# TensorE's order in a fused token, attention and FFN kernel: two instead of three regions of array halves, and the first FFN product one step later

## The chip, the cores and the metric

One core of a Trainium2 chip runs the whole program. The metric is the device time of one execution in microseconds (us), median of several runs. The profiled execution has a time of its own, and its span (first to last instruction) lies within that time. TensorE is PE, its weight loader PEld, VectorE is DVE, ScalarE is ACT, GpSimd is POOL, and SyncE is SP, whose queue (SPq) issues the DMAs.

## What is computed

The input x is 64 sequences of 256 rows of 192 numbers, f32. Three layers follow each other, the last two with a residual and a layer norm ahead of them:

```python
h = tok(x, tok_Wq, tok_bq, tok_Wkv, tok_bkv)   # per sequence: 16 blocks of 16 rows; 8 queries, keys, values
                                               # per block, softmax of 8 x 8, out = q + attn v -> 128 rows
h = h + attn(layernorm(h), Wq, Wk, Wv, Wo)     # 12 heads of 64, 3 key/value heads, rope, softmax; 64 x 128
                                               # rows make (64, 128, 192), each sequence attends within itself
h = h + gelu(layernorm(h) @ in_weight.T + in_bias) @ out_weight      # 192 -> 768 -> 192
```

The output is 64 x 128 x 192.

## The kernel before, in words

The 64 sequences are worked on in 32 pairs (NP = 32). Every engine runs the same software pipeline: step p does the attention of pair p (att), the token layer of pair p + 1 (tok), the end of the attention and the FFN of pair p - 1 (ffn), and the second FFN product of pair p - 2 (fin). Steps -1, 0 and 1 fill the pipe, steps 2 to 30 are the loop, steps 31 to 33 empty it. The order of the work on each engine is written out by hand, in that engine's function step; the engines meet by semaphores alone, so an engine that waits holds up all that stands behind it.

The names that matter, for PE: qk_projected(0..3) and v_projected project queries, keys and values (f32r matmuls of 256 columns, 10 to each part); tok_qk projects the token layer from x_sb and waits for x_loaded; tok_scores, tok_mix and tok_h are the rest of the token layer; scores(a) are the attention scores of sequence a of the pair, probs_v(a) its value product, output(a) the product with Wo; x_turned and hn_turned transpose the normalised rows; ffn_first and ffn_second are the FFN's products. scores uses halves of the array's rows; probs_v, tok_scores and tok_h use halves of its columns; all else uses the full array. A "region of array halves" is an uninterrupted stretch of such matmuls.

On ACT stand the exponentials (score_exp), copies out of PSUM (v_out_of_psum, heads_out, h_added), gelus, and the first part of each f32r split (x_hi, h_hi). On DVE: the rotations' first half (rotate), key_max, the second part of each split (x_lo, h_lo), the norms, and blocks_turned(a, k), which transposes 32 x 32 blocks of the probabilities E into EB. On POOL: the rotations' second half (8 pieces to a pair), the normalisation of the probabilities (probs), the powers of the norms.

Probabilities must be transposed for the value product. DVE turns the blocks, SP writes EB to a DRAM buffer (3 spills), waits for them to land and reads them back in block order into ET (8 loads); this is blocks_moved(a, q). The x of the next pair has one buffer, x_sb: load_ahead(n) waits until tok_h of pair n - 1 has read it. In a loop step SP runs these in this order:

```python
blocks_moved(1, p - 1)
blocks_moved(0, p)
load_ahead(p + 2)
store(p - 2)
```

In blocks_moved all three spills stand ahead of the first load of ET, so the loads wait for blocks_turned(a, 2) to be done as well. PSUM has eight banks: two rings of three (RING[0], RING[1]) and B6, B7. Which product may run where is set by who still reads a bank: tok_qk writes into RING[1], whose second bank also holds the last two of the six hidden blocks (HIDDEN[2]), so it waits for gelus.

In the loop, PE's step 2 to 30 before is: projections 0 and 1, tok_qk, projections 2 and 3, values; one piece of ffn_second; probs_v(0), tok_scores, scores(0); output(0); probs_v(1); a piece; tok_mix; output(1); pieces; tok_h, scores(1); a piece; hn_turned; pieces; ffn_first(0), x_turned, ffn_first(2, 1).

Of the kernel before, what the change touches and what calls it, by code (L numbers as in the profile page):

```python
# [63 lines left out]
GELU_ORDER = (4, 5, 0, 1, 2, 3)  # L64
FFN_BANKS = {True: (0, 2, 1), False: (0, 1, 2)}
# [25 lines left out]
def program(nc, x, w_tok, b_tok, bq_row, bv_row, w_att1, w_att2, wo, w_in1, w_in2, b_in, w_out,  # L91
# [4 lines left out]
    with ExitStack() as ctx:  # L96
# [10 lines left out]
        TOK_S, TOK_M, TOK_H = RING[1][:, 512 + DP:512 + DP + P], B7[:, 0:DP], RING[0][:, 512:512 + 2 * D]  # L107
# [6 lines left out]
        FIRST_T = (B6[:], B7[:], RING[0][:, 1024:1536])  # L114
# [41 lines left out]
        v_tok, v_late, OT = sb("v_tok", [P, 2, DKV]), sb("v_late", [P, DKV]), sb("OT", [P, 2, DQ])  # L156
# [10 lines left out]
        s_keys = sem("s_keys")  # L167
# [26 lines left out]
        norm_out, first_mm, first_out = sem("norm_out"), sem("first_mm"), sem("first_out")  # L194
# [39 lines left out]
        def _(sp):  # L234
# [40 lines left out]
            def step(p, att, ffn, fin, more):  # L275
                if ffn and not (isinstance(p, int) and p == NP):
                    blocks_moved(1, p - 1)
                if isinstance(p, int) and p == 0:
                    for k in range(3):
                        sp.sem_inc(spilled[k], 16)  # L280
                    for k in range(2):
                        sp.sem_inc(filled[k], 64)
# [11 lines left out]
            for dst, src in ((smask, c_mask), (ident, c_ident), (rope_kc, c_rope_kc), (rope_ks, c_rope_ks),  # L294
# [16 lines left out]
        def _(act):  # L311
# [13 lines left out]
            def step(p, att, tok, ffn, fin):  # L325
                n = p + 1
                att_first = isinstance(p, int) and p == 0
                att_last = isinstance(p, int) and p == NP - 1
                main = att and fin
# [16 lines left out]
                def v_out_of_psum():  # L346
                    need(act, pv_mm, 4 * (p - 1) + 2)
# [24 lines left out]
                def first_copied(k):  # L372
                    g = GROUPS[k]
                    s0, heads = PIECES[g // 2]
                    h0 = REP * g - s0
                    act.wait_ge(first_mm, k + 1)
                    nc.scalar.copy(
                        ET[:, 0, s0 * P:(s0 + heads) * P].rearrange("p (i h c) -> p h i c", i=NB, h=heads)[:, h0:h0 + REP],
                        FIRST_T[k].rearrange("p (h i c) -> p h i c", h=REP, i=NB)).then_inc(first_out, 1)

# [13 lines left out]
                def v_kept_late():  # L394
                    act.wait_ge(v_out, p + 1)
                    need(act, pv_mm, 4 * p)
                    nc.scalar.copy(v_late[:], v_tok[:, 1]).then_inc(v_kept, 1)
# [14 lines left out]
                def exp_warmed():  # L412
                    act.wait_ge(s_warm_exp, p + 1)
                    nc.scalar.activation(warm[:, 1:2], half_neg[:, 0:1], ACT.Exp).then_inc(s_warm_exp, 1)

                def gelus():
                    act.wait_ge(s_warm, p)
                    nc.scalar.activation(warm[:, 0:1], warm[:, 0:1], ACT.Gelu).then_inc(s_warm, 1)
                    for m in GELU_ORDER if att else range(NM):
                        act.wait_ge(hid_mm, 3 * (p - 1) + FFN_BANKS[main].index(m // 2) + 1)  # L420
# [3 lines left out]
                if main:  # L424
                    exp_warmed()
                    bias_summed()
                    v_out_of_psum()
                    heads_out(p - 1, HEADS_0)
                    if tok:
                        token_exp()  # L430
                    for k in range(NKV):
                        score_exp(0, k)
                    residual_kept()
                    if tok:
                        h_added()
                    v_kept_late()
                    h_normalised()
                    residual_moved()
                    h_hi()
                    score_exp(1, 0)  # L440
                    score_exp(1, 1)
# [972 lines left out]
```

## Time and profile before

| | us |
|---|---|
| median of 3 runs | 946.08 (945.1 to 946.31) |
| the profiled execution's own time | 945.8 |
| its span | 943.8 |
| PE busy | 914.4 (97% of the span) |
| DVE / ACT / POOL busy | 761.9 / 639.6 / 666.1 |
| TensorE's granted clock, mean | 0.994 |

The rows below come from three kinds of view. A row of the timeline gives the start and the length of an instruction or of a group of like ones (x12 is twelve), and in brackets how long the engine was idle before it and who released it. Matmuls overlap their neighbours, so the distance from one start to the next is what a matmul takes of PE's time, not its length. A row of the stretches gives the busy time of each engine in a stretch, and the clock granted in it (1.00 is 2.4 GHz, 0.50 is 1.2 GHz). A row of the waits gives who waited for whom, in total, with count and longest.

### The profile page before, as it was taken

How to read it: one execution, taken by the hardware profiler on the slowest of the kernel's cores; microseconds unless marked ns; L12 is line 12 of the kernel's file. 1: busy time of each engine (PE TensorE's matmuls, PEld its weight loads, DVE VectorE, ACT ScalarE, POOL GpSimd, SP SyncE). 2: the span in 40 equal slices, each digit the busy share in tenths (PEclk: the TensorE clock that was granted, in tenths of full speed). 3: DMA queues.
4: the chain of work that ended last, by engine and by line, in shares of the span. 5: the costliest groups of instructions: out<-in, count | busy, mean ns of one | idle time of the engine just before them, and what ended most of it. 6: DMA issues, size and time to landing. Idle time of an engine off the chain costs nothing.

```text
span 943.8 us, 26528 instructions
## 1 busy us (share of the span) xinstructions
PE 914.4 (97%) x7722; PEld 799.7 (85%) x7722; DVE 761.9 (81%) x1999; ACT 639.6 (68%) x2501; POOL 666.1 (71%) x968
## 2 busy tenths in 40 slices
PE   5779999999999999999999999999999999999998
PEld 3567998888998888988888889888899888899877
DVE  3787888888888888888888888888888888888863
ACT  2556676667677667677667768666767766767763
POOL 2686677787667787667777767777766778766771
PEclk8999999999999999999999999999999999999999
DMA  6034644445545444554444554444564444555440
GB/s 205 24 91 135 165 126 126 131 121 153 164 138 131 122 131 134 164 149 134 116 127 131 162 161 123 126 131 126 153 164 132 130 126 126 141 164 147 114 118 21
DMA packets 193424, 124.63 MB, mean 132 GB/s; under 512 B 30976, under 2 KB 184960, under 8 KB 193408
## 3 DMA queue, kind: packets, MB, share of 16 engines
q1 hardware_dynamic: 190528, 121.02, 46.8%
q10 hardware_dynamic: 2880, 3.41, 1.1%
q8 instruction: 8, 0.13, 0.1%
q14 instruction: 8, 0.07, 0.0%
HBM read 69.32 MB, written 55.05 MB: 132 GB/s over the span
## 4 chain that ended last, share of the span: by engine, by line
PE 93%; DVE 3%; issue 1%; ACT 1%; DMA 1%; POOL 1%; SPq 0%; ACTq 0%; DVEq 0%; POOLq 0%
PE ring L1043 15%; PE bank L1062 14%; PE ring L1081 11%; PE bank L1260 7%; PE ring L1260 6%; PE ring L1117 6%; PE ring L1161 5%; PE ring L1021 4%; PE ring L1167 3%; PE bank L1117 3%; PE ring L1186 3%; PE ring L1221 3%; PE bank L1161 2%; PE ring L1198 2%; PE bank L1167 2%; PE bank L1242 2%
## 5 line engine op out<-in xcount | busy, mean ns | idle before, releaser
L335 ACT ACTIVATE E<-ring,m_neg 128x128 f32<-128x128 f32 x768 | 270.5, 384 | 17.3 <-DVE m_neg L688 16.9
L546 POOL TENSOR_TENSOR E<-E,e_rcp 128x512 f32<-128x512 f32 x158 | 177.8, 1126 | 85.6 <-DVE e_rcp L711 83.1
L538 POOL TENSOR_TENSOR qkT<-rot_c,rot_s 128x256 f32<-128x256 f32 x256 | 187.3, 732 | 20.1
L335 ACT ACTIVATION_READ_ACCUMULATOR E<-ring,m_neg 128x1 f32 x768 | 171.0, 223 | 0.0
L536 POOL TENSOR_TENSOR rot_s<-rot_s,rope_qs 128x256 f32<-128x256 f32 x192 | 143.3, 746 | 20.2 <-DVE rot_s L682 20.2
L1062 PE MATMUL bank<-wout_sb,G 128*128 128x192 f32 x744 | 152.0, 334 | 0.0
L688 DVE TENSOR_REDUCE m_neg<-ring 128x4 f32<-128x512 f32 x192 | 127.4, 678 | 21.3 <-PE ring L1081 21.3
L1062 PEld LDWEIGHTS bank<-wout_sb,G 128*128 128x128 f32 x744 | 118.7, 190 | 15.2 <-issue 11.5
L702 DVE STREAM_TRANSPOSE EB<-E 128x512 f32<-128x512 f32 x186 | 126.0, 692 | 1.6 <-POOL E L546 0.8
L1081 PE MATMUL ring<-qkT 64*128 64x128 f32 x1536 | 103.0, 280 | 2.2 <-POOL qkT L538 0.7
L1081 PEld LDWEIGHTS ring<-qkT 64*128 64x128 f32 x1536 | 91.6, 187 | 14.6 <-issue 13.1
L349 ACT COPY v_tok<-ring 128x384 f32<-128x384 f32 x32 | 15.3, 479 | 118.2 <-PE ring L1117 111.7
L682 DVE STREAM_SHUFFLE rot_s<-ring 128x512 f32<-128x512 f32 x128 | 94.6, 739 | 0.0
L355 ACT COPY h_next<-ring 128x384 f32<-128x384 f32 x32 | 15.3, 479 | 97.6 <-PE ring L1221 97.5
L680 DVE TENSOR_TENSOR rot_c<-ring,rope_qc 128x512 f32<-128x512 f32 x96 | 65.4, 681 | 16.9 <-PE ring L1043 16.9
L1043 PE MATMUL ring<-XH,WH 128*128 128x256 f32 x256 | 74.9, 293 | 1.9 <-ACT XH L410 1.4
L536 POOL TENSOR_TENSOR rot_s<-rot_s,rope_ks 128x256 f32<-128x256 f32 x64 | 46.6, 729 | 38.8 <-DVE rot_s L682 38.7
L1043 PE MATMUL ring<-XL,WH 128*128 128x256 f32 x256 | 71.7, 280 | 0.8 <-DVE XL L771 0.8
L1043 PE MATMUL ring<-XH,W2S 128*128 128x256 f32 x256 | 71.6, 280 | 0.0
L1043 PE MATMUL ring<-XL,W2S 128*128 128x256 f32 x256 | 71.6, 280 | 0.0
L1043 PE MATMUL ring<-XH,WL 128*128 128x256 f32 x256 | 71.5, 279 | 0.0
L1260 PE MATMUL bank<-wo_sb,OT 128*128 128x192 f32 x384 | 70.8, 334 | 0.7 <-ACT OT L343 0.7
(160 smaller groups left out, 2476.8 us busy)
## 6 DMA issues: line engine op xcount, KB each, us to landing
spill<-EB SPq DMA_DIRECT2D x186, 256.0 KB, 2.3
ET<-spill SPq DMA_DIRECT2D x248, 128.0 KB, 2.8
ET<-spill SPq DMA_DIRECT2D x248, 64.0 KB, 2.4
x_sb<-in_x_dram SPq DMA_DIRECT2D x64, 192.0 KB, 2.5
out_dram<-out_sb SPq DMA_DIRECT2D x31, 192.0 KB, 2.5
x_sb<-in_x_dram SPq DMA_DIRECT2D x64, 64.0 KB, 2.4
w_raw<-in_w_att_dram ACTq DMA_DIRECT2D x2, 608.0 KB, 5.2
win_raw<-in_w_in_dram ACTq DMA_DIRECT2D x2, 384.0 KB, 6.4
```

The lines of the kernel that those rows point to most:

```text
L335: last = nc.scalar.activation(E[:, a, s * P:(s + 1) * P], RING[a][:, s * P:(s + 1) * P], ACT.Exp, bias=m_neg[:, a, s:s + 1], accum_out=e_s ...
L536: nc.gpsimd.tensor_tensor(rot_s[:, b, :, a], rot_s[:, b, :, a], sin, ALU.mult).then_inc(sin_out, 1)
L538: nc.gpsimd.tensor_tensor(qkT[:, b, :, a], rot_c[:, b, :, a], rot_s[:, b, :, a], ALU.add).then_inc(q_out, 1)
L546: nc.gpsimd.tensor_tensor(e, e, r, ALU.mult).then_inc(prob_out, 1)
L682: nc.vector.stream_shuffle(rot_s[:, b].rearrange("p c a t -> p (c a t)"), src, SWAP).then_inc(rot_out, 1)
L688: nc.vector.tensor_reduce(m_neg[:, a, REP * g:REP * (g + 1)], RING[a][:, 512 * g:512 * (g + 1)].rearrange("p (h k) -> p h k", k=P), AX_X, ...
L702: nc.vector.transpose(EB[:, a, s0 * P:(s0 + heads) * P].rearrange("p (j h c) -> p h j c", j=NB, h=heads)[:, h0:h0 + REP], E[:, a, 512 * g: ...
L1043: last = nc.tensor.matmul(RING[0][:, 512 * (i % 2) + half * DP:512 * (i % 2) + (half + 1) * DP], w[:, c], r, start=(k == 0), stop=(k == 4))
L1062: last = nc.tensor.matmul(y, G[:, m, a * P:(a + 1) * P], wout_sb[:, m, :], start=(m == 0), stop=(m == NM - 1))
L1081: last = nc.tensor.matmul(RING[a][:, s * P:(s + 1) * P], qkT[rows, t // 2, t % 2, a], qkT[rows, 3, h // 8, a], start=True, stop=True)
L1117: last = nc.tensor.matmul(dst[k * HD:(k + 1) * HD], v[:, g * HD:(g + 1) * HD], src.rearrange("p i h c -> p i (h c)"), start=True, stop=True)
L1260: last = nc.tensor.matmul(y, OT[:, a, t * P:(t + 1) * P], wo_sb[:, t, :], start=(t == 0), stop=(t == 5))
```

## The change

It moves work on every engine. The second FFN product of pair p - 2 stays in step p; the first one (and the gelus) of pair p - 2 now also stand in step p, at its head, where before they stood at the end of step p - 1. x_turned moves ahead of the last pieces of ffn_second, tok_qk behind v_projected, the second values are split in two around tok_h, and the second output follows scores(1). The values of both sequences (v_late was one, is now two) are kept a step longer, and the late products get other banks. The first and the last steps follow the same list; fillers (kept_warm, matmuls of zeros into a bank that nothing reads) stand in the first ones, and the first pair's probabilities are no longer transposed on PE but go through DRAM like all others. On SP the one difference is that step 0 loads ahead before it moves blocks; the loop's order is as above.

The core of the diff (PE's new list, which has no second copy for special steps; ACT's and DVE's parts that the prediction speaks of):

```diff
-        ATT_Y, ATT_Y0, ATT_YB = RING[1][:, 1024:1024 + D], B6[:, 0:D], B7[:, 0:D]
+        ATT_Y, LATE_Y = RING[1][:, 1024:1024 + D], (RING[1][:, 512:512 + D], RING[0][:, 512:512 + D])
-        HEADS_0 = (B7[:], RING[1][:, 1024:1024 + DP])
+        LATE_HEADS = ((RING[1][:, 1024:1536], B7[:, 0:DP]), (B7[:], RING[0][:, 0:DP]))
...
+                early = isinstance(p, int) and p == 0
+                if more and early:
+                    load_ahead(p + 2)
-                elif att:
+                if att:
                     blocks_moved(0, p)
-                if more:
+                if more and not early:
                     load_ahead(p + 2)
...
+                if fin:
+                    gelus()
+                if att and ffn:
+                    v_kept_late()
...
                 if att:
                     qk_projected(0)
                     qk_projected(1)
+                if fin and not (isinstance(p, int) and p == NP):
+                    ffn_first(p - 2)
+                if att:
                     qk_projected(2)
                     qk_projected(3)
                     v_projected()
+                if tok:
+                    tok_qk()
+                if first in ("tok", "att"):
+                    kept_warm(2)
+                if fin:
+                    ffn_second(0, p - 2, range(1))
+                if att and ffn:
+                    probs_v(0, p - 1, 0, late=True)
+                    probs_v(0, p - 1, 1, late=True)
...
+                if tok:
+                    tok_mix()
...
+                if att and ffn:
+                    probs_v(1, p - 1, 0, late=True)
+                if tok:
+                    tok_h()
+                if att and ffn:
+                    probs_v(1, p - 1, 1, late=True)
...
+                if att:
+                    scores(1)
+                if att and ffn:
+                    output(1, p - 1, late=True)
...
+                if fin:
+                    ffn_second(0, p - 2, range(1, 3))
+                if tok:
+                    x_turned()
...
+                if fin:
+                    ffn_second(0, p - 2, range(3, NM))
+                    ffn_second(1, p - 2)
+                if ffn:
+                    hn_turned()
+                if att_last:
+                    probs_v(0, p, 0)
+                    probs_v(0, p, 1)
+                    ffn_first(p - 1)
```

How rows stand on the engines. First PE, in a loop step, around tok_qk (the two products from x_sb, L1182 and L1186); before:

```order
L1043 MATMUL ring<-XL,W2S 128x256
L1175 ISA
L1177 REGISTER_ALU [waits x_loaded]
L1179 ISA [waits exp_out]
L1182 MATMUL ring<-bd_qk,x_sb 128x2x64 [waits gelu_out]
L1182 MATMUL ring<-bd_qk,x_sb 128x2x64
L1186 MATMUL ring<-bd_qk,x_sb 128x2x64 x4
L213 ISA
L1043 MATMUL ring<-XH,WH 128x256 [waits rot_out]
L1043 MATMUL ring<-XH,WL 128x256
```

and after (L1015 and L1019 are tok_qk, L870 the values' projection, L961 the first values):

```order
L870 MATMUL ring<-XL,W2S 128x256
L1008 ISA
L1010 REGISTER_ALU [waits x_loaded]
L1012 REGISTER_ALU [waits exp_out]
L1015 MATMUL ring<-bd_qk,x_sb 128x2x64 [waits gelu_out]
L1015 MATMUL ring<-bd_qk,x_sb 128x2x64
L1019 MATMUL ring<-bd_qk,x_sb 128x2x64 x4
L913 MATMUL bank<-wout_sb,G 128x192 [waits gelu_out]
L953 ISA [waits exp_out,v_kept]
L961 MATMUL ring<-ET,v_late 64x512 [waits filled_01]
```

tok_qk moved from behind the second projection to behind the last, 60 matmuls of 256 columns later, and still waits for x_loaded. Then DVE, in a loop step, around the last two turns of the first sequence's blocks (EB<-E, with spilled_0 and spilled_2); before:

```order
L784 TENSOR_TENSOR t_m<-bank,bd_qk 128x256 [waits h_mm,m_mm]
L749 TENSOR_TENSOR h<-ring,h_cur 128x192 [waits y_mm,h_kept1]
L844 BN_STATS st<-h 128x6 [waits h2_out]
L700 ISA
L702 STREAM_TRANSPOSE EB<-E 128x4x4x32 [waits spilled_0,prob_out]
L840 BN_AGGR mv<-st 128x2 [waits ln2_st]
L702 STREAM_TRANSPOSE EB<-E 128x4x4x32 [waits spilled_2,prob_out]
L663 TENSOR_SCALAR hn<-h,mv,rs 128x192 [waits hT_mm,ln2_rs]
```

and after:

```order
L699 TENSOR_TENSOR XL<-bank,XH 128x512 [waits XH_out]
L596 TENSOR_SCALAR hn<-h,mv,rs 128x192 [waits hT_mm,ln2_rs]
L598 TENSOR_SCALAR hn<-h,mv,rs 128x64
L622 REGISTER_ALU
L623 TENSOR_REDUCE m_neg<-ring 128x4 [waits sc_mm]
L635 ISA
L637 STREAM_TRANSPOSE EB<-E 128x4x4x32 [waits spilled_0,prob_out]
L646 RECIPROCAL e_rcp<-e_sum 128x4 [waits exp_out]
L210 REGISTER_ALU [waits ffn_mm]
L694 TENSOR_TENSOR out_sb<-bank,h_kept 128x384 [waits h2_copied,stored]
L635 REGISTER_ALU
L637 STREAM_TRANSPOSE EB<-E 128x4x4x32 [waits spilled_2,prob_out]
```

Both turns moved from ahead of hn's normalisation to behind it, behind x_lo and the last key maximum, and the second also behind the FFN's result.

## Rows read from the trace of the kernel before

**Rows 1.** Stretches: span of time, length, busy of PE, PEld, DVE, ACT, POOL, clock
```profile
107.73:892.97 785.24, 783.81 (x6723) 691.52 (x6722) 660.95 (x1737) 556.76 (x2185) 579.29 (x840) 1.00 0.50 138
...
57.00:62.00 5.00, 2.58 (x45) 2.31 (x43) 3.67 (x11) 1.13 (x5) 4.36 (x7) 1.00 0.75 210
...
70.00:78.00 8.00, 6.42 (x38) 5.95 (x38) 6.45 (x18) 5.04 (x26) 3.05 (x6) 0.79 0.75 199
```

**Rows 2.** Timeline of SP's queue at the end of a loop step
```profile
494.30 3.65 SPq L257 DMA_DIRECT2D ET<-spill  x8
498.22 0.40 SPq L238 DMA_DIRECT2D x_sb<-in_x_dram  x1
...
499.96 0.37 SPq L239 DMA_DIRECT2D x_sb<-in_x_dram  x1
```

**Rows 3.** The tile x_sb: time from a DMA's issue to its landing
```profile
DMA to landing us min/median/max: 2.2/2.5/2.7
```

**Rows 4.** Timeline of PE in a loop step, and the next step's tok_qk
```profile
474.75 0.60 PE L1182 MATMUL ring<-bd_qk,x_sb 128*128 128x128 f32 x4
...
476.00 0.36 PE L1043 MATMUL ring<-XH,WH 128*128 128x256 f32 x1
...
479.60 0.48 PE L1062 MATMUL bank<-wout_sb,G 128*128 128x192 f32 x2
480.01 1.08 PE L1117 MATMUL bank<-ET,v_tok 128*64 128x512 f32 x4
...
483.73 2.22 PE L1260 MATMUL bank<-wo_sb,OT 128*128 128x192 f32 x12
485.88 1.51 PE L1117 MATMUL ring<-ET,v_late 128*64 128x512 f32 x8
...
487.75 0.61 PE L1211 MATMUL bank<-t_aT,bd_v 128*128 128x128 f32 x4
488.19 2.12 PE L1260 MATMUL ring<-wo_sb,OT 128*128 128x192 f32 x12
...
491.21 0.87 PE L1221 MATMUL ring<-x_sb,t_m 128*64 128x192 f32 x8
...
502.88 0.71 PE L1182 MATMUL ring<-bd_qk,x_sb 128*128 128x128 f32 x4
```

**Rows 5.** Waits: who waited for what, in total, times, longest
```profile
PEld ring L1117 <- issue: 41.6, 153, 0.3
```

**Rows 6.** Timeline of ACT and DVE: h_next in a loop step, and in step -1
```profile
492.26 0.48 ACT L355 COPY h_next<-ring 128x384 f32<-128x384 f32 x1 [3.16 <-PE ring L1221]
...
19.90 0.48 ACT L355 COPY h_next<-ring 128x384 f32<-128x384 f32 x1 [4.44 <-PE ring L1221]
...
22.71 0.38 DVE L663 TENSOR_SCALAR xn<-h_next,mv,rs 128x192 f32<-128x192 f32 x1 [1.29 <-POOL rs L560]
```

**Rows 7.** Timeline of DVE in a loop step
```profile
490.42 0.36 DVE L749 TENSOR_TENSOR h<-ring,h_cur 128x192 f32<-128x192 f32 x1 [0.51 <-PE ring L1260]
490.81 0.36 DVE L844 BATCH_NORM_STATS2 st<-h 128x6 f32<-128x192 f32 x1
491.09 0.69 DVE L702 STREAM_TRANSPOSE EB<-E 128x512 f32<-128x512 f32 x1
...
495.85 0.68 DVE L688 TENSOR_REDUCE m_neg<-ring 128x4 f32<-128x512 f32 x1
496.44 0.37 DVE L663 TENSOR_SCALAR xn<-h_next,mv,rs 128x192 f32<-128x192 f32 x1
...
497.47 0.17 DVE L711 RECIPROCAL e_rcp<-e_sum 128x4 f32<-128x4 f32 x1
```

**Rows 8.** Timeline of PE: first matmul of steps 0 and 1, and the last step's values
```profile
25.09 0.36 PE L1043 MATMUL ring<-XH,WH 128*128 128x256 f32 x1 [0.77 <-ACT XH L410]
...
49.65 0.42 PE L1043 MATMUL ring<-XH,WH 128*128 128x256 f32 x1
...
919.48 1.51 PE L1117 MATMUL ring<-ET,v_tok 128*64 128x512 f32 x8
```

More of the change, by code:

```diff
@@ L450, in step @@
-                if att and not att_first:
-                    exp_warmed()
+                if att and fin:
+                    exp_warmed()
+                if att and ffn:
+                    heads_out(p - 1, LATE_HEADS[0])
+                if tok:
+                    token_exp()
+                if starts:
+                    act.wait_ge(s_w2, 16 * 2)
+                    nc.scalar.copy(WH1[:], w_raw1[:]).then_inc(s_hi, 1)
+                    nc.scalar.copy(W2S[:], w_raw2[:]).then_inc(s_hi, 1)
@@ L608, in step @@
                         probs(1, k, p)
[L609 removed]
+                if ffn:
+                    residual_copied()
+                if starts:
                     pool.wait_ge(s_hi, 4)
@@ L957, in step @@
+                if att:
+                    key_max(1, (0,))
+                    sums_inverted(0, 2, p)
+                if tok:
+                    x_normalised()
+                if att:
+                    blocks_turned(0, 0, p)
                 if ffn:
                     dve.wait_ge(h_kept[1], p)
-                    attention_added(1, 2 * p)
-                if att and not att_first:
-                    sums_inverted(0, 2, p)
-                if ffn:
+                    attention_added(1, 2 * p, late=att)
@@ L963, in step @@
                     spread(1, 2 * p)
-                if att and not att_first:
-                    blocks_turned(0, 0, p)
-                if ffn:
                     variance(1, 2 * p)
-                if att and not att_first:
-                    blocks_turned(0, 1, p)
-                    blocks_turned(0, 2, p)
+                if att:
+                    key_max(1, (1,))
+                if tok:
+                    x_lo()
                 if ffn:
@@ L1130, in last_probs_turned @@
+                    for k, (g, src) in enumerate(halves):
+                        last = nc.tensor.matmul(dst[k * HD:(k + 1) * HD],
+                                                v[:, g * HD:(g + 1) * HD], src.rearrange("p i h c -> p i (h c)"),
+                                                start=True, stop=True)
+                    last.then_inc(pv_mm, 1)
                 def last_probs_turned(k):
                     g = GROUPS[k]
-                    pe.wait_ge(prob_out, 5 * p + 3 + k - 2)
+                    pe.wait_ge(prob_out, 5 * p + 3 + k)
@@ L1326, in step @@
                     scores(0)
-                if ffn and not ends:
-                    probs_v(1, p - 1)
+                if att and ffn:
+                    output(0, p - 1, late=True)
                 if first == "tok":
                     kept_warm(3)
-                if fin:
-                    ffn_second(0, p - 2, range(2, 4))
+                if first == "att":
+                    kept_warm(3)
                 if tok:
-                    if first == "tok":
-                        pe.wait_ge(s_const, 16 * 6)
@@ L1336, in step @@
                     tok_mix()
-                if ffn and not ends:
-                    output(1, p - 1)
-                if tok and not fin:
+                if first == "tok":
+                    kept_warm(1)
+                if att and ffn:
+                    probs_v(1, p - 1, 0, late=True)
+                if tok:
                     tok_h()
+                if att and ffn:
+                    probs_v(1, p - 1, 1, late=True)
                 if first == "tok":
-                    kept_warm(4)
```

542 lines of the change are left out of this document (151 added, 391 removed).

## The prediction, made before the changed kernel was run

> **What bounds the kernel now.** I read the stretches first, then TensorE's timeline of one step, then the timelines of the engines and of SyncE's queue around the loads of x. In the 28 loop steps from 107.73 to 892.97 us PE is busy 783.81 of 785.24 us at a granted clock of 1.00, so a step lasts 28.04 us and is a gapless row of matmuls [rows 1]. Only work taken off PE's row can shorten it; any wait put into the row lengthens it one for one. The second thing to see is SyncE: it issues everything in one order, and in a step the x of a later pair comes last, behind the eight ET loads (494.30), at 498.22 to 499.96; a load of x lands after a median 2.5 us [rows 2, 3]. That is about 502.5, and the token product tok_qk that reads it started at 502.88, 0.1 us later than its place after 20 matmuls asked for [rows 4]. So x is already within half a microsecond of being the wait that ends last.
>
> **The change, part by part.**
>
> PE's gain. No matmul of a loop step is added or removed. Before, a step entered array halves three times (first values and scores; second values; tok_h and scores); after, twice. The whole price of the entries is bounded by the idle of PE's weight loader at the value products: 41.6 us in 153 idles, 0.27 each, two of them per region and step [rows 5]. One region fewer is then worth 0 to 0.54 us of PE time a step. I take 0.4: the group of the output product spans 2.22 us (at 483.73) between two regions and 2.12 (at 488.19) among full matmuls, so 0.1 shows there, and each drained edge is an idle of 0.27; the value lies nearer the upper bound, since a region has both edges [rows 4, 5]. Step without any wait: 28.04 - 0.4 = 27.6 us. The Trainium skill, page "TensorEngine Tiling (Array Packing)", section "Tiling Modes", says that a change of tiling mode drains the engine; by that rule the change would simply be faster, which is the first rival below.
>
> The moved first FFN product. Its 30 matmuls now stand between the second and the third projection (0.12 us each, as 30 took 476.00 to 479.60 [rows 4]); it needs HH and HL of the previous step, which come in the first microseconds. The gelus follow it on ACT with both table loads and are done some 2.5 us before tok_qk needs all six. v_late is now copied for both halves (a tenth more on ACT); the first values' and outputs' new banks cost nothing. I cost these at nothing: ACT is busy 557 of 785 us [rows 1].
>
> The moved token product and its wait on x. tok_qk now stands 80 instead of 20 matmuls into the step (9.6 instead of 2.4 us). But what SyncE waits for before it may issue x has moved further: blocks_turned(0, 1) and (0, 2) on DVE stood before hn's normalisation; now they stand behind x_lo, hn and the last key maximum. From tok_qk of one step to tok_qk of the next there is now a closed chain, all of it on rows:
> - tok_qk, PE, to the start of tok_h: tok_qk 1.25 (474.75 to 476.00); first FFN piece, first values, token scores, scores and output 6.28 (479.60 to 485.88); tok_mix 0.44; second values, first piece 0.91 (the group at 480.01 spans 1.08, and its last matmul overlaps what follows by 0.17). Sum 8.88 [rows 4].
> - tok_h's start to h_next on ACT: 1.05 (491.21 to 492.26). h_next to x_normalised with nothing between: 2.81 (19.90 to 22.71) [rows 4, 6].
> - DVE from x_normalised to the end of blocks_turned(0, 1): 1.03 for xn (496.44 to 497.47), 0.62 blocks_turned(0, 0) (its 0.69 less the usual overlap of 0.07), 0.39 attention_added, 0.28 spread, 0.2 variance (an estimate: small, but it waits for spread), 0.59 key_max, 0.65 x_lo (as large as a key_max), 0.6 hn (two operations like half of xn's four), 0.59 key_max, 0.69 blocks_turned. Sum 5.64 [rows 7]. XH and the rstd of hn arrive 0.2 to 0.3 us before DVE asks for them, so DVE runs through.
> - SyncE: end of blocks_turned(0, 1) (491.09 + 0.69) to the first ET load 2.52; eight ET loads 3.92 (to 498.22); four x loads, last issued 1.74 later; landing 2.5; 0.1 to PE. Sum 10.78 [rows 2, 3, 7].
>
> Cycle: 8.88 + 1.05 + 2.81 + 5.64 + 10.78 = **29.16 us**, against 27.6 for PE's own row. PE then stands still for 1.5 us ahead of tok_qk in every step. Nothing in it shortens when PE is late, since every link starts from tok_qk. The Trainium skill, page "DMA: Bandwidth & Descriptors", section "Anatomy of one DMA — SWDGE (gpsimd) path", gives a fixed cost of about 2.0 us per DMA; with that in both landings the cycle would be 28.2 and the time about 952. The trace shows 2.5 [rows 3], and that decides.
>
> I also followed the other waits of the new step at PE's pace. The closest are the token scores (DVE's token_qk ends 0.1 to 0.2 us ahead), hn_turned (0.35), tok_h (0.35), x_turned (0.5), scores (1.8 or more, behind the rotations). Second values: ET is filled 2 us ahead. None waits.
>
> The head. Step -1 no longer puts the weight copy ahead of the token exponential and the mask has its own semaphore; I put step 0 at 22 instead of 25.09 us. Step 0 drops 12 transposes, the first values and an output, and ends at 44 instead of 49.65 [rows 8]. Step 1 has no FFN matmuls to cover DVE's tail, and its tok_qk comes 7 us in, at 51. The fillers run only in idle time. tok_qk of step 2 stands one cycle later, at 80; bounds of the head 76 to 84.
>
> The tail. From the start of step 31 to the end it was 943.8 - 892.97 = 50.8 us, of which 24.3 after probs_v(0) began at 919.48 [rows 1, 8]. In the new last step PE takes probs_v(0, 31) right behind hn_turned, at 25.3 us; blocks_turned(0, 1) ends at about 25.5 and from there to the first half of ET it is 2.5 to the first load, 2 for four loads and a landing that I put at 3.5 (x's is 2.5 and ET's packets are smaller, an estimate), so probs_v starts at about 33.5: an 8 us hole. Behind it come the 24.3 us plus the first FFN product of pair 30 (3.6, before it was ahead of probs_v) and 0.6 for HH, no longer covered. A clock that falls to its lower level after the hole adds 1.6: from 70 to 78 us, after PE's idle spells in step 1, it was 0.79 in the mean, 8 x 0.21 = 1.7 us lost [rows 1]. Sum 33.5 + 24.3 + 3.6 + 0.6 + 1.6 = 63.6. Bounds 55 to 67.
>
> Sum against the profiled execution (span 943.8, its own time 945.8, 2.0 around the span; the median of the three runs is 946.08, 0.3 above it): tok_qk of step 2 at 80, 28 cycles of 29.16 = 816.5, to tok_qk of step 30 at 896.5; to step 31's start 27.6 - 9.6 = 18.0; tail 63.6; 2.0 around: **980 us**.
>
> **Rivals.**
> 1. PE keeps setting the pace (the other side, faster). The one mechanism: x lands by 9.6 us after a step's start, because the chain is shorter than I add up. For it: the chain is a sum of some twenty pieces, and SyncE held the same order before without a wait. Against it: it must be 1.6 us short, and its largest pieces (6.28, 3.92, 2.52) are read off whole. Time: 78 + 28 x 27.6 + 18.0 + 63.6 + 2.0 = 934. It decides at a cycle of 27.9: below that the kernel is faster.
> 2. The chain sets the pace, but is 0.5 to 1.1 us shorter (ET loads or landings quicker than read): cycle 28.0 to 28.6, time 948 to 964.
> 3. The standstill in each step also drops the clock to its lower level. Price: the 1.7 us lost from 70 to 78, once a step: 28 x 1.7 = 48 more, 1028 us. Against: PE was busy only 2.58 of the 5 us from 57 to 62 and stayed at 1.00 [rows 1].
> 4. The change does not do what it says: the second region is broken up by tok_h's wait. Then PE's row stays 28.0, hidden below the chain: 980 as well.
>
> **How the numbers follow.** Forecast with its own range 964 to 996 (28 cycles of 28.6 to 29.7, and the ends): 0.72. Rival 1: 0.14. Rival 2: 0.09. Rival 3: 0.03. Rival 4: 0.02, counted with the forecast's time. The range of 8 in 10 takes the forecast and rival 2 down to 950, and ends of the head and tail up to 1000. A measurement of this kernel can tell about 0.2% from no change. Faster 0.14 (rival 1), within 0.2% 0.03 (the edge of rivals 1 and 2), slower 0.83.
>
> **What would show it.** In the profile after: PE idle about 1.5 us ahead of the first matmul of tok_qk in every loop step, released by the DMA of x_sb; loop steps of 29.2 us; PE busy share near 94%; SyncE's x loads issued about 24.9 to 26.6 us after the tok_qk of the same step; blocks_turned(0, 1) ending 18.4 us after it; a hole of about 8 us ahead of the last step's probs_v; clock 1.00 in the loop. What would make me wrong: tok_qk starting right behind v_projected (rival 1), or another wait, such as scores or hn_turned, standing ahead of it in the list of waits. If the loop step is 27.6 and the total still above 940, the tail is the error.

## The result, and the profile after

The changed kernel took 982.57 us (median of 4 runs, 981.41 to 984.17), beside 946.19 us (945.1 to 948.49) for the kernel before on the same chip: 1.038 times the time, 95% interval 1.036 to 1.040. The forecast was 980 us, slower, with a range of 950 to 1000. Its profiled execution has a span of 981.3 us. Ratios, here and below, leave out runs over 1.5% above the fastest of the same kernel, which are two of the four of store_first and none elsewhere.

The stretches of the changed kernel, columns as in [rows 1] (from the start of the loop's second step, step 3, to the middle of step 31, and one step from tok_qk to tok_qk):

```profile
113.00:930.00 817.00, 780.99 (x6741) 699.75 (x6741) 651.32 (x1739) 574.97 (x2189) 573.50 (x845) 1.00 0.48 134
463.59:492.60 29.01, 27.81 (x240) 24.94 (x240) 23.23 (x62) 20.38 (x79) 20.32 (x31) 1.00 0.47 133
```

Before, PE was busy 783.81 of 785.24 us [rows 1]; now it is idle for 36 of 817 us at the same clock. Who it waits for is in its list of waits (engine, tile and line, then the releaser: total, times, longest):

```profile
PE ring L1015 <- DMA x_sb<-in_x_dram: 38.9, 29, 3.3
PE ring L961 <- DMA ET<-spill: 7.1, 1, 7.1
PE ring L894 <- DVE rot_s L617: 3.5, 2, 3.1
```

L1015 is tok_qk: one wait in each step from 2 to 30, of 3.3 us in step 2 and of 1.27 us in the mean of the other 28 (1.34 over all). The other two rows are mainly one hole in step 31 and one in step 1. The shares of the chain of waits that ended last, by engine:

```profile
PE 36%; DVE 17%; DMA 15%; SPq 15%; issue 9%; POOL 5%; ACT 2%; DVEq 0%; ACTq 0%; POOLq 0%
```

PE no longer carries the span. It shares it with DVE, SyncE's queue and transfers, which is the closed chain of the prediction. The chain in rows, from the timelines of PE, ACT, DVE and SP, in the order of time:

```profile
463.59 0.71 PE L1015 MATMUL ring<-bd_qk,x_sb 128*128 128x128 f32 x4 [1.27 <-DMA x_sb<-in_x_dram]
...
472.53 0.82 PE L1050 MATMUL ring<-x_sb,t_m 128*64 128x192 f32 x8
...
473.53 0.48 ACT L350 COPY h_next<-ring 128x384 f32<-128x384 f32 x1 [0.62 <-PE ring L1050]
...
476.33 0.38 DVE L596 TENSOR_SCALAR xn<-h_next,mv,rs 128x192 f32<-128x192 f32 x1
...
480.68 0.68 DVE L623 TENSOR_REDUCE m_neg<-ring 128x4 f32<-128x512 f32 x1
481.28 0.70 DVE L637 STREAM_TRANSPOSE EB<-E 128x512 f32<-128x512 f32 x1
...
484.38 3.64 SPq L254 DMA_DIRECT2D ET<-spill  x8
488.29 0.40 SPq L235 DMA_DIRECT2D x_sb<-in_x_dram  x1
...
490.03 0.37 SPq L236 DMA_DIRECT2D x_sb<-in_x_dram  x1
...
492.72 0.71 PE L1015 MATMUL ring<-bd_qk,x_sb 128*128 128x128 f32 x4 [1.32 <-DMA x_sb<-in_x_dram]
```

Link by link, forecast against measured: tok_qk to tok_h 8.88 and 8.94; tok_h to the normalised x 3.86 and 3.80; DVE from there to the end of blocks_turned(0, 1) 5.64 and 5.65 (481.28 + 0.70 - 476.33); to the first ET load 2.52 and 2.40; the ET loads 3.92 and 3.91; the x loads 1.74 and 1.74; landing and PE's start 2.6 and 2.69 (2.48 to 2.76 over the 28 steps from step 3). The step is 29.07 us in the mean of 27 (870.59 - 85.82 for the starts of tok_qk in steps 2 and 29), where 29.16 was forecast. Every release in the chain is visible, but that the chain closes through SyncE's order, and not through something that moves with it, had to be tested.

### The profile page after: what moved, and what is told of

Read it like the earlier page. It is cut to its first block, busy times and chain, and to the rows that moved or that the text cites. A ratio compares the mean times of both kernels' runs of the same rounds, so it can differ in the third digit from the quotient of the medians.

```text
span 981.3 us, 26749 instructions
## 1 busy us (share of the span) xinstructions
PE 921.3 (94%) x7754; PEld 813.5 (83%) x7754; DVE 751.3 (77%) x2000; ACT 655.1 (67%) x2496; POOL 657.4 (67%) x970
## 4 chain that ended last, share of the span: by engine, by line
PE 36%; DVE 17%; DMA 15%; SPq 15%; issue 9%; POOL 5%; ACT 2%; DVEq 0%; ACTq 0%; POOLq 0%
SPq L254 10%; DMA x_sb<-in_x_dram 7%; PE ring L1089 7%; DMA spill<-EB 7%; PE ring L932 5%; PE bank L961 4%; PE ring L961 3%; SPq L235 3%; PE ring L1019 3%; DVE m_neg L623 3%; POOL rs L508 2%; DVE EB L637 2%; PE ring L1015 2%; PE ring L1050 2%; DVE st L720 2%
## 5 line engine op out<-in xcount | busy, mean ns | idle before, releaser
L494 POOL TENSOR_TENSOR E<-E,e_rcp 128x512 f32<-128x512 f32 x160 | 166.2, 1040 | 126.8 <-DVE e_rcp L646 124.3
L484 POOL TENSOR_TENSOR rot_s<-rot_s,rope_qs 128x256 f32<-128x256 f32 x192 | 140.7, 733 | 32.7 <-DVE rot_s L617 32.6
L330 ACT ACTIVATION_READ_ACCUMULATOR E<-ring,m_neg 128x1 f32 x768 | 162.1, 211 | 0.0
L1089 PE MATMUL ring<-wo_sb,OT 128*128 128x192 f32 x756 | 139.8, 335 | 0.0
L913 PE MATMUL bank<-wout_sb,G 128*128 128x192 f32 x744 | 135.8, 326 | 0.0
L637 DVE STREAM_TRANSPOSE EB<-E 128x512 f32<-128x512 f32 x189 | 131.3, 698 | 1.0 <-POOL E L494 1.0
L1089 PEld LDWEIGHTS ring<-wo_sb,OT 128*128 128x128 f32 x756 | 121.1, 190 | 7.9 <-issue 0.4
L913 PEld LDWEIGHTS bank<-wout_sb,G 128*128 128x128 f32 x744 | 120.4, 190 | 0.0
L932 PE MATMUL ring<-qkT 64*128 64x128 f32 x1536 | 103.0, 281 | 1.2 <-POOL qkT L486 1.2
L932 PEld LDWEIGHTS ring<-qkT 64*128 64x128 f32 x1536 | 90.7, 188 | 16.1 <-issue 11.8
L735 DVE TENSOR_TENSOR qkT<-ring,bqk_row 128x512 f32<-128x512 f32 x32 | 22.1, 692 | 81.5 <-PE ring L1019 81.5
L338 ACT COPY OT<-ring 128x512 f32<-128x512 f32 (+1 forms) x33 | 19.1, 578 | 74.1 <-PE ring L961 74.1
```

Of the source, the lines that this page charges most:

```text
L330: last = nc.scalar.activation(E[:, a, s * P:(s + 1) * P], RING[a][:, s * P:(s + 1) * P], ACT.Exp, bias=m_neg[:, a, s:s + 1], accum_out=e_s ...
L484: nc.gpsimd.tensor_tensor(rot_s[:, b, :, a], rot_s[:, b, :, a], sin, ALU.mult).then_inc(sin_out, 1)
L494: nc.gpsimd.tensor_tensor(e, e, r, ALU.mult).then_inc(prob_out, 1)
L637: nc.vector.transpose(EB[:, a, s0 * P:(s0 + heads) * P].rearrange("p (j h c) -> p h j c", j=NB, h=heads)[:, h0:h0 + REP], E[:, a, 512 * g: ...
L913: last = nc.tensor.matmul(y, G[:, m, a * P:(a + 1) * P], wout_sb[:, m, :], start=(m == 0), stop=(m == NM - 1))
L932: last = nc.tensor.matmul(RING[a][:, s * P:(s + 1) * P], qkT[rows, t // 2, t % 2, a], qkT[rows, 3, h // 8, a], start=True, stop=True)
```

## The experiments

In all runs below the kernel before had a median of 949 to 950 us, 0.4% above its runs beside the changed kernel. So differences between two experiments are taken from their medians and from the steps in their traces. Where one is compared with the changed kernel the steps decide, and the ratios show the same sign.

**x_early.** The x loads go ahead of the first sequence's blocks in every step, not in step 0 alone:

```diff
-                early = isinstance(p, int) and p == 0
+                early = True
```

> The changed kernel with one edit on SyncE: load_ahead stands ahead of blocks_moved(0, p) in every step, as it already does in step 0. Theory (a closed chain tok_qk - tok_h - norm - blocks_turned(0, 1) - spill - ET loads - x loads - tok_qk of 29.07 us sets the step): x then lands some 15 us before it is read, PE no longer waits ahead of tok_qk (38.9 us in 29 waits vanish), the loop step is 27.7 us, the total 982.6 - 38.9 - about 2 = 940 to 944, just below the kernel before. Rival A (x's wait only hides another one that is nearly as long, such as scores, hn_turned or ET): another wait of 0.5 to 1.3 us a step takes its place, total 960 to 980. Rival B (the x loads in their new place hold back the spills and ET): PE waits for ET ahead of the values, total unchanged or longer.

Measured: 939.04 us (938.54 to 940.21), 0.988 of before (0.986 to 0.991). The wait on x_sb is gone from the list but for 0.5 us at the very start. From one tok_qk to the next it is 27.58 us (497.29 to 524.87), and the stretch of the loop is PE's again:

```profile
113.00:890.00 777.00, 776.49 (x6754) 698.90 (x6756) 659.19 (x1741) 575.93 (x2201) 575.97 (x847) 1.00 0.51 140
```

The standstill is SyncE's order of transfers, and PE waits for nothing else in the loop. With that one line the change is a gain, by the pace of 27.6 us that the first rival named.

**before_x_early.** The same order of SP's queue on the kernel before, where x was not waited for:

```diff
                     blocks_moved(1, p - 1)
+                if more:
+                    load_ahead(p + 2)
...
                 elif att:
                     blocks_moved(0, p)
-                if more:
-                    load_ahead(p + 2)
```

> The kernel before with the same edit as x_early: load_ahead ahead of blocks_moved(0, p) in every step. Theory (before, PE alone set the step, and x landed just in time): no change, within 0.3% of 946. Rival (SyncE's queue already cost something in each step, as the 0.1 us ahead of tok_qk hints): up to 3 us faster. If SyncE, waiting for tok_h, holds back the spills: slower.

Measured: 948.18 us (945.37 to 950.94), 0.998 (0.996 to 1.000). Loading x early gains next to nothing by itself (0.2%; its loop step is 28.01 us, where it was 28.04); the gain of x_early is not that of the loads alone.

**store_first.** The result's store ahead of the x loads, so one more transfer stands in the chain:

```diff
-                if more and not early:
-                    load_ahead(p + 2)
                 if fin:
                     store(p - 2)
+                if more and not early:
+                    load_ahead(p + 2)
```

> The changed kernel with the store of the output put ahead of the four x loads on SyncE, one DMA issue (0.58 us) more in the chain in steps 2 to 29. Theory (the chain is closed and has no slack): every loop step longer by 0.58 us, 28 x 0.58 = 16 us, total 998 to 999. Rival (x's wait is a symptom that slack elsewhere absorbs): less than 5 us.

Measured: 1015.13, 1028.1, 1030.9 and 1031.31 us, at mean granted clocks of 0.976, 0.963, 0.962 and 0.962; the ratio is 1.075 (1.069 to 1.082), from the first two alone. That is 16 to 33 us more than this theory gave. The trace is of the run of 1030.9 us. The mechanism did what was expected: the store stands 0.67 us ahead of the first x load, the wait on x_sb is 58.8 us in 29 waits, 2.03 each and 0.69 more than without the edit, and the 10 steps in which the clock stays at 1.00 last 29.77 us in the mean, 0.70 more than the changed kernel's. The rest is the clock, which fell at the end of the wait or just behind it in the other 18 of the 28 steps; these last 31.22 us. PE's timeline at tok_qk in four steps (the second and the third with a fall), and stretches (the first without a fall, then two with one, then 1 us of a fall, then another step without one):

```profile
362.03 0.71 PE L1015 MATMUL ring<-bd_qk,x_sb 128*128 128x128 f32 x4 [1.98 <-DMA x_sb<-in_x_dram]
...
391.87 0.97 PE L1015 MATMUL ring<-bd_qk,x_sb 128*128 128x128 f32 x4 [2.13 <-DMA x_sb<-in_x_dram]
...
483.84 0.80 PE L1015 MATMUL ring<-bd_qk,x_sb 128*128 128x128 f32 x4 [1.87 <-DMA x_sb<-in_x_dram]
...
791.74 0.71 PE L1015 MATMUL ring<-bd_qk,x_sb 128*128 128x128 f32 x4 [2.09 <-DMA x_sb<-in_x_dram]
```

```profile
362.03:391.87 29.84, 27.71 (x241) 24.97 (x241) 23.06 (x62) 20.58 (x79) 20.52 (x32) 1.00 0.47 130
391.87:422.00 30.13, 29.26 (x240) 26.30 (x240) 23.06 (x62) 19.27 (x77) 19.19 (x29) 0.94 0.45 119
483.84:515.11 31.27, 29.27 (x241) 26.15 (x241) 23.06 (x62) 20.59 (x80) 20.48 (x31) 0.94 0.46 124
...
392.80:393.80 1.00, 1.00 (x7) 1.00 (x6) 0.00 (x0) 0.00 (x0) 1.00 (x2) 0.50 0.73 260
...
791.74:821.47 29.73, 27.71 (x241) 24.97 (x241) 23.06 (x62) 20.42 (x79) 20.31 (x31) 1.00 0.47 130
```

The same four matmuls span 0.71 us at 2.4 GHz and 0.80 or 0.97 us where the clock falls among them. A step with a fall holds 29.26 us of PE work instead of 27.71, 1.5 us more, at a mean granted clock of 0.94. The clock fell behind the gap of 1.87 us and not behind that of 2.09 us, so the gap's length alone does not decide. This is the prediction's third rival: it does not act at the changed kernel's 1.3 us, and at 2.0 it acts in 18 steps of 28.

**turn_first.** The changed kernel with one DVE operation less ahead of blocks_turned(0, 1); SP's order is untouched:

```diff
                 if att:
-                    key_max(1, (2,))
                     blocks_turned(0, 1, p)
+                    key_max(1, (2,))
                     sums_inverted(1, 0, p)
```

> The changed kernel (982.6 us) with one edit on DVE: the last two turns of the first sequence's blocks stand so that blocks_turned(0, 1) comes ahead of the last key maximum (0.6 us) instead of behind it. SP's order is as in the changed kernel. Theory (the step is the closed chain from tok_qk over h_next, DVE, the spills, ET and x back to tok_qk): the chain gets shorter by one key maximum, 0.55 to 0.65 us, each of the 28 steps too, 982.6 - 16.8 = 965 to 967; the wait on x falls from 1.34 to about 0.75 us a step. Rival (DVE's place of the turn does not set when x is issued, only the number of transfers ahead of it does): no change, 981 to 984.

Measured: 966.0 us (963.86 to 967.51), 1.018 (1.015 to 1.021). PE's timeline at three tok_qk:

```profile
454.57 0.71 PE L1015 MATMUL ring<-bd_qk,x_sb 128*128 128x128 f32 x4 [0.77 <-DMA x_sb<-in_x_dram]
...
483.00 0.71 PE L1015 MATMUL ring<-bd_qk,x_sb 128*128 128x128 f32 x4 [0.71 <-DMA x_sb<-in_x_dram]
...
511.40 0.71 PE L1015 MATMUL ring<-bd_qk,x_sb 128*128 128x128 f32 x4 [0.70 <-DMA x_sb<-in_x_dram]
```

Over the 28 steps from tok_qk of step 2 the step is 28.46 us in the mean, 0.61 less than the changed kernel's, one key maximum; the wait is 0.74 instead of 1.27. DVE is busy for 78% of this kernel, so it is not what one would call the bottleneck, yet the place of one 0.6 us operation on it was worth 17 us of the total (28 x 0.61; the medians differ by 16.6), because it stood in a chain that closes on itself. x_early takes the x loads out of the chain and the wait is gone; store_first lengthens SyncE's link by an issue of 0.67 us and the step grows by 0.70 where the clock holds; turn_first shortens DVE's link by 0.6 us and the step shrinks by 0.61. That settles the cause.

**tail_ffn_first.** The changed kernel; in step 31 the first FFN product of pair 30 runs in the hole ahead of the value product, the last transposes stay behind it:

```diff
                 if att_last:
+                    ffn_first(p - 1)
                     probs_v(0, p, 0)
                     probs_v(0, p, 1)
-                    ffn_first(p - 1)
```

> The changed kernel with one edit in PE's step 31: the first FFN product of pair 30 ahead of the values of pair 31 instead of behind them. Theory (PE stands still 7.1 us for ET there): the 3.6 us of the product move into the hole, the hole shrinks to 3.5, total shorter by 3.6 to 5 us (the clock may fall less), about 978. Rival (the hole is followed by work that is late anyway): under 1 us.

Measured: 978.92 us (978.28 to 980.17), 1.030 (1.028 to 1.033); the span is 3.1 us shorter, the wait for ET 1.9 instead of 7.1 us. The hole is real, and 5 us of it are filled, by the product and its own wait of 0.68 us for HH. From the start of the value product to the end it is 25.3 instead of 30.4 us, 5.1 less for 3.6 us of moved matmuls, since the clock no longer falls there. The rest of that gain is hidden in the span: tok_qk of step 30 stands 2.1 us later in this trace (901.81 against 899.67), 1.5 of them in step 2, where the clock fell behind the gap of 2.7 us (0.72 from 84 to 90 us) and in the changed kernel's trace did not fall behind one of 3.3 us.

**early_and_tail.** x_early, and in step 31 also the last transposes ahead of the value product:

```diff
                 if att_last:
-                    probs_v(0, p, 0)
-                    probs_v(0, p, 1)
                     ffn_first(p - 1)
                     for k in range(3):
                         last_probs_turned(k)
+                    probs_v(0, p, 0)
+                    probs_v(0, p, 1)
                     last_pair = True
```

> x_early (939.0 us) with one more edit in step 31: the first FFN product of pair 30 and the last transposes ahead of the last step's value product, in the time in which PE waited 7.0 us for ET. Theory (the hole in the last step is time in which PE has other work at hand, and the two edits are independent): 939.0 less the 3.7 us that the same edit gave on the changed kernel (982.6 to 978.9), so 935 to 936; the wait of PE for ET in the last step falls from 7.0 to about 2 us. Rival (with x early the last step's hole is bounded by something else, such as gelu or the FFN's result): 938 to 939. The loop step stays at 27.6 us, with no wait on x_sb.

Measured: 931.87 us (930.38 to 932.76), 0.981 (0.979 to 0.984); 7.2 us less than x_early where 3 to 4 were expected. In all 5.1 us of work (30 matmuls at 0.12 and the transposes' 1.5) went into the hole, and the gain is larger than that. The difference is the clock. Here is one stretch of x_early around the end of its 7.0 us hole, and one of early_and_tail at the same place:

```profile
905.00:910.00 5.00, 3.02 (x9) 1.07 (x10) 0.00 (x0) 0.74 (x2) 0.00 (x0) 0.50 0.45 125
```

```profile
904.00:909.00 5.00, 4.44 (x32) 2.81 (x30) 1.98 (x3) 0.67 (x2) 0.12 (x1) 1.00 0.65 192
```

With the hole filled the clock does not fall. The second sequence's value product starts at 909.34 instead of 916.84 us.

**third_region.** x_early, with two pieces of the second FFN product between the last value product and scores(1), so that a step enters the array halves three times again:

```diff
                     probs_v(1, p - 1, 1, late=True)
+                if fin:
+                    ffn_second(0, p - 2, range(1, 3))
...
                     output(1, p - 1, late=True)
-                if fin:
-                    ffn_second(0, p - 2, range(1, 3))
```

> x_early (939.0 us) with two pieces of the second FFN product put between the last value product and scores(1), so that a step enters the array halves three times again, as before the change; nothing else moves. Theory (the loop step fell from 28.04 to 27.58 us because one region of array halves less has to be entered and left): the step goes back up by 0.3 to 0.5 us, the total by 9 to 14 us to 948 to 953. Rival (the 0.46 us came from the rest of the new order, such as the placement of the transposes or of the first FFN product): the step stays within 0.1 us of 27.58 and the total within 3 us of 939.

Measured: 945.45 us (944.07 to 946.15), 0.996 (0.994 to 0.998); 6.4 us above x_early, between theory and rival. Two tok_qk of it:

```profile
500.52 0.61 PE L1015 MATMUL ring<-bd_qk,x_sb 128*128 128x128 f32 x4
...
528.30 0.61 PE L1015 MATMUL ring<-bd_qk,x_sb 128*128 128x128 f32 x4
```

The step is 27.78 us, 0.20 more. This third region of array halves costs 0.2 us. It is not quite the one of before: counted as changes between the full array, halves of its columns and halves of its rows (`128*128`, `128*64` and `64*128` in PE's timeline), a step has 8 before, 6 in x_early and 7 here. The other 0.26 of the 0.46 us between the steps before (28.04) and of x_early (27.58) is the eighth change or something else. The weight loader's idles that differ between the two (rows of the waits, from 113 to 890 us: x_early, then this run):

```profile
PEld ring L932 <- issue: 10.8, 28, 0.4
```

```profile
PEld bank L913 <- issue: 10.8, 28, 0.4
...
PEld ring L932 <- issue: 6.3, 28, 0.2
```

L913 is the moved piece, L932 is scores(1) behind it. Together that is 0.22 us of idle more in a step (6.3 / 28), about what PE's step grew by.

**v_last.** x_early with the values' projection behind tok_qk: the step's one row of f32r matmuls is broken by f32 ones.

```diff
-                    v_projected()
                 if tok:
                     tok_qk()
+                if att:
+                    v_projected()
```

> x_early (939.0 us, step 27.58) with the values' projection behind tok_qk instead of ahead of it; the same matmuls. The step's one row of f32r matmuls (projections, first FFN product, values: 80 in a row) is then broken once by the 6 f32 matmuls of tok_qk. third_region gave back only 0.20 us of the 0.46 us by which the step of x_early is shorter than the step before. Theory (the rest, 0.26 us, is the price of going from f32 products to f32r ones and back, which the kernel before did three times in a step and the new order does once): the step gets longer by 0.10 to 0.18 us, to 27.68 to 27.76, the total by 3 to 5 us to 942 to 944, and the first f32r matmul behind tok_qk stands 0.2 instead of 0.12 us from the second. Rival (the order of f32 and f32r products costs nothing, the rest came from elsewhere): the step stays within 0.03 us of 27.58 and the total within 1 us of 939.

Measured: 937.13 us (936.67 to 939.46), 0.987 (0.984 to 0.989). The theory fell. PE's timeline around tok_qk:

```profile
494.37 0.60 PE L1015 MATMUL ring<-bd_qk,x_sb 128*128 128x128 f32 x4
494.81 1.06 PE L1019 MATMUL ring<-bd_qk,x_sb 128*128 128x128 f32 x8
495.63 0.37 PE L870 MATMUL ring<-WH,XH 128*128 128x256 f32 x1
495.83 0.28 PE L870 MATMUL ring<-WL,XH 128*128 128x256 f32 x1
...
521.96 0.60 PE L1015 MATMUL ring<-bd_qk,x_sb 128*128 128x128 f32 x4
```

The first f32r matmul does stand 0.20 us from the second (0.08 more), but tok_qk ahead of it takes 1.26 instead of the 1.33 us it takes ahead of an f32 product (497.29 to 498.62 in x_early), and the step is 27.59. The order of the two types costs nothing net. The total is 1.9 us below x_early's, outside the rival's 1 us too; that difference lies in the head, where step 2 starts at 72.34 instead of 73.98 us (see all_three). Where the 0.26 us are can be read by setting the same groups of both steps beside each other (before [rows 4] against x_early):

```profile
499.04 1.08 PE L961 MATMUL ring<-ET,v_late 128*64 128x512 f32 x4
499.95 0.60 PE L961 MATMUL bank<-ET,v_late 128*64 128x256 f32 x4
500.38 0.32 PE L1031 MATMUL ring<-qkT 128*64 128x64 f32 x4
...
500.99 1.61 PE L932 MATMUL ring<-qkT 64*128 64x128 f32 x24
```

The first values and the token scores up to scores(0) took 2.18 us before (480.01 to 482.19) and take 1.95 now (499.04 to 500.99). Third_region has 1.34 and 0.60 us for the two, so the number of regions is not behind it. Outside these two groups the step is 25.86 us before, 25.63 in x_early and 25.84 in third_region: there the third region gives back nearly all, so little is left for an eighth change. (Single groups differ by up to 0.2 us in both directions, tok_mix by 0.20 more and the first FFN product by 0.22 less; only the sums are compared.) The token scores' part goes with the weight loader's waits for the keys from DVE, 0.39 us a step before and 0.27 in x_early (rows of the waits, from 113 to 890 us: before, then x_early):

```profile
PEld ring L1198 <- DVE kT L812: 10.9, 28, 0.4
```

```profile
PEld ring L1031 <- DVE kT L740: 7.6, 28, 0.3
```

That is 0.12 us by which weights of the token scores wait less. It is not that they have more time behind tok_qk: they start 3.1 us behind it in x_early and 6.7 us before, and why DVE's keys come in time is open. The other 0.1 lies in the first values. No run isolates either, so these are readings, not shown causes.

**no_fillers.** x_early without the matmuls of zeros in steps -1, 0 and 1, but for one:

```diff
-                    for _ in range(count):
+                    for _ in range(1 if first == 'tok' and count == 4 else 0):
```

> x_early (939.0 us) without the matmuls of zeros (the fillers) in steps -1, 0 and 1, but for one in step -1. Theory (the fillers run in time in which PE is idle anyway and keep the granted clock up in the head, where projections would else run at the lower level): step 2 starts 1 to 4 us later, the total is 940 to 943, the clock between 15 and 60 us has more stretches below 1.00; the loop step stays 27.6. Rival (the fillers stand in PE's way or bring nothing): 937 to 939, with the same clock in the head.

Measured: 943.65 us (941.87 to 945.03), 0.994 (0.992 to 0.996); 4.6 us above x_early, 2.9 by the spans. The token product of step -1 behind x's landing, without fillers and with them (x_early), shows what they do:

```profile
6.39 1.20 PE L1015 MATMUL ring<-bd_qk,x_sb 128*128 128x128 f32 x4 [3.44 <-DMA x_sb<-in_x_dram]
```

```profile
6.43 0.68 PE L1015 MATMUL ring<-bd_qk,x_sb 128*128 128x128 f32 x4 [0.54 <-DMA x_sb<-in_x_dram]
```

Both start together, and the first takes nearly twice as long, the lower clock against the higher. (The level is read from the lengths alone; the stretches of this trace list 1.00 for 5 to 10 us.) tok_h starts 2.2 us later (16.34 against 14.17), and step 0 at 24.8 instead of 21.8 us. That is nearly the 25.09 of before [rows 8], which had 18 such matmuls against 62 in x_early and 2 here: the fillers make up almost the whole gain at this place.

**all_three.** early_and_tail and v_last together.

> early_and_tail (931.9 us) and v_last together: x early, the first FFN product ahead of the last step's value product, and the values' projection behind tok_qk. Theory (v_last's 1.9 us below x_early lie in the head: with tok_qk 1.2 us earlier PE's gap in step 1 starts 0.7 us sooner, and the projections behind it ran at 0.72 instead of 0.50 of the clock; the loop is the same): 930 to 931. Rival (that difference was which clock the gap in step 1 happened to meet): 931.5 to 932.5. No wait on x_sb and a step of 27.58 in both.

Measured: 930.71 us (930.41 to 932.0), 0.980 (0.978 to 0.982), the fastest of all. The loop is the same. The head's stretch behind the gap of 3.1 us in step 1, in x_early and here:

```profile
50.00:56.00 6.00, 5.68 (x26) 5.68 (x27) 4.44 (x11) 0.00 (x0) 4.35 (x6) 0.50 0.91 248
```

```profile
50.00:56.00 6.00, 6.00 (x40) 5.99 (x39) 4.72 (x12) 0.00 (x0) 5.13 (x8) 0.72 0.78 217
```

The gap is as long as in x_early, but less of the work behind it meets the lower clock. v_last shows the same 0.72. But so does the changed kernel itself, with the gap at the same place and tok_qk still behind the values:

```profile
50.00:56.00 6.00, 5.77 (x36) 5.77 (x37) 4.72 (x11) 0.40 (x1) 4.55 (x7) 0.72 0.87 242
```

Store_first, turn_first and tail_ffn_first have 0.72 too, and early_and_tail and third_region 0.50 or 0.51 like x_early. So the place of tok_qk isn't shown to be what decides between the two; the rival, that it is which clock the gap happens to meet, stands. The difference to early_and_tail (1.2 us, on two chips) is smaller than the spread of either kernel's runs.

## Why the prediction was right, point by point

- **The bound moves from PE to the chain.** Right, and shown by three edits of the chain. The sum of some twenty pieces was 29.16 and the step is 29.07; over 28 cycles that is 2.5 us less.
- **Landing of a DMA.** The trace's 2.5 us for x [rows 3] held (2.48 to 2.76 with PE's start). The spill's way through memory measured 2.40 us to the next issue; so the profile's own figure was the one to use. With 2.0 for both landings, the figure of the Trainium skill's page "DMA: Bandwidth & Descriptors", section "Anatomy of one DMA — SWDGE (gpsimd) path", the cycle would have been 28.2, an estimate; the page gives it for DMAs that GpSimd issues, and here SyncE issues them.
- **Everything else at nothing.** Right in the loop as far as PE's waits show: x_early has none there once x's is gone. The weight loader is less free: in x_early it waits 0.45 us a step for ACT ahead of tok_h (before, 0.23 us of idle stood there) and 0.17 us for DVE ahead of tok_mix (before, none). No run isolates what these cost in PE's row; the step of 27.58 us holds them.
- **PE's own row.** 27.6 was forecast and 27.58 is measured, but for a reason half wrong, so the closeness is in part luck. The region was put at 0.4 us; the one of third_region is worth 0.20. The upper bound of 0.54 rested on a misreading of [rows 5]: the 153 idles of 0.27 us are five in a step, and four of the five stand between matmuls of one value product. Only one is at an edge. The second values before, the idle at the edge and the first of the inner ones:

```profile
485.88 0.20 PEld L1117 LDWEIGHTS ring<-ET,v_late 128*64 128x64 f32 x4 [0.23 <-issue]
486.36 0.14 PEld L1117 LDWEIGHTS ring<-ET,v_late 128*64 128x64 f32 x2 [0.29 <-issue]
```

  The other 0.26 us, which the sum didn't hold, lie for the most part in the first values and the token scores.
- **The head.** This is the mis-sized term: tok_qk of step 2 stood at 85.82 instead of 80 us, outside the bounds of 76 to 84. Steps 0 and 1 started as forecast (21.71 and 44.14), though the 3 us of step 0 are nearly all the fillers' doing (no_fillers), where the prediction gave them to the moved weight copy and said of the fillers only that they run in idle time: the number was right there for another reason. Step 1 then lost time in two ways that the 7 us "into the step" left out:

```profile
50.23 0.58 PE L894 MATMUL ring<-XH,WH 128*128 128x256 f32 x1 [3.12 <-DVE rot_s L617]
50.61 0.42 PE L894 MATMUL ring<-XH,WL 128*128 128x256 f32 x1
...
53.58 0.28 PE L894 MATMUL ring<-XH,WH 128*128 128x256 f32 x1
53.70 0.28 PE L894 MATMUL ring<-XH,WL 128*128 128x256 f32 x1
```

  This is the changed kernel's PE in step 1. Its third projection waited 3.12 us for DVE's rotations. The matmuls behind it stood 0.21 us apart instead of 0.12 until 53.4. tok_qk(1) came at 55.34 and not at 51. The cycle from there was 30.48 instead of 29.16, since that step's eight ET loads took 5.25 us to issue and not 3.65.
- **The tail.** 63.6 us forecast, 63.6 measured (917.68 to 981.3). The exact match is luck: PE reached the hole at 26.1 us into the step instead of 25.3, the hole was put at 8 us and is 7.1, and what follows it was put at 30.1 us and is 30.4.
- **The sum.** Head 5.8 more, cycles 2.5 less: 983 against 980 forecast.
- **The rivals.** That the chain is short by 1.6 us (rival 1) or by 0.5 to 1.1 us (rival 2) is out, by the step of 29.07 us. Rival 3 was rightly out at 1.3 us; it is near, as store_first shows. Rival 4 is out: PE's own row in x_early is 27.58 and not 28.0.

## What to carry to other kernels

Before moving a product to another place in the row of the bounding engine, follow its input backwards through the in-order queues until the path ends or returns to the product itself; if it returns, the length of the loop is a pace of its own, and every operation in it costs its full length in each step, on whichever engine. A row of idle times bounds a price only after one has looked where in the step the idles stand. Here the remedy was one line, the x loads ahead of eight others that nobody was in such a hurry for. Give the holes at the start and the end of the program whatever work is at hand, and price them with the clock: 5.1 us of work moved into a hole gave 7.2.

## What the runs showed of the hardware that was not expected

- A step with a gap of 1.3 us on PE kept 2.4 GHz through all 28 steps of the changed kernel. With gaps of 1.8 to 2.2 us (2.9 in step 2) in otherwise the same steps (store_first) the clock fell to 1.2 GHz in 18 of 28 steps: in 391.87 to 422.00 a step holds 1.5 us more of PE time. It fell behind a gap of 1.87 us and not behind one of 2.09 us; in step 2 it fell behind 2.88 us (store_first) and stayed at 1.00 behind 3.30 us (the changed kernel). What decides beside the length isn't shown. One DMA issue more, which lengthened the gap by 0.69 us, cost 33 to 49 us over the four runs; in the traced one 20 of them are the chain (28 x 0.70) and about 26 the clock (18 x 1.45).
- One more region of array halves, cut out of another (one change of halves more, third_region), costs 0.20 us a step (5.6 us of 939); the weight loader's idle grows by 0.22. Alternating f32 and f32r products costs nothing net: 0.08 us more at one edge, 0.07 less at the other.
- Fillers on an idle PE shortened a latency-bound head by about 3 us, with 60 matmuls of zeros in the trace.
